# Fetching edge lists a slot earlier, releasing slots exactly, and adding three bf16 parts in PSUM, in a graph attention kernel on one core

## The reference

```python
def _gat_layer(x, W, al, ar, b, src, dst, apply_act):
    h = (x @ W).reshape(N_NODES, HEADS, HEAD_DIM)
    el = einsum('nhd,hd->nh', h, al); er = einsum('nhd,hd->nh', h, ar)
    e = leaky_relu(el[src] + er[dst], 0.2)
    ex = exp(e - segment_max(e, dst)[dst])
    a = ex / segment_sum(ex, dst)[dst]
    out = segment_sum(h[src] * a[:, :, None], dst) + b
    return leaky_relu(out, 0.01) if apply_act else out
```

## Time and profile before

| what | value |
|---|---|
| median of 3 runs | 9250.0 us (9241.39 to 9254.71) |
| the profiled execution | 9270.94 us, span of its instructions 9269.2 us |
| PE busy, PEld, DVE, ACT, POOL | 65%, 50%, 51%, 18%, 49% |
| mean granted clock of TensorE | 0.80 |
| pairs of layer 0, 1, 2 | us 182 to 2930, 2955 to 5645, 5673 to 9210 |
| L358 gathers | x4716, 4542.2 us busy on POOL |
| L1285 aggregation | x10560 matmuls, 3761.3 us on PE |
| L992 msg, L1000 sel, L979 sum of parts | 1658.2, 906.2, 466.5 us on DVE, x1320 each |

### The profile page before, as it was taken

The page is one execution under the profiler, slowest core; times in us unless marked ns, Lnnn a source line. Parts: engine busy times, 40 slices in busy tenths (PEclk is TensorE's granted clock), DMA queues, the critical chain, the costliest instruction groups (busy, mean ns, idle before and its releaser), DMA issues.

```text
span 9269.2 us, 139557 instructions
## 1 busy us (share of the span) xinstructions
PE 6004.1 (65%) x27934; PEld 4636.2 (50%) x27935; DVE 4741.8 (51%) x10724; ACT 1700.8 (18%) x4763; POOL 4543.3 (49%) x4723
## 2 busy tenths in 40 slices
PE   4555555555665555555565665566777778888888
PEld 2334434444444344444444453345556666767777
DVE  5445555555555445555555564454544444444444
ACT  2000000000110000000000000012333444445454
POOL 1655555555554665555555554555444433333332
PEclk8677778778787677777777776678888999999999
DMA  5444444434443444444443444443333322222221
GB/s 177 114 111 111 111 108 113 106 103 104 108 107 95 116 111 113 109 108 111 107 111 99 104 108 95 110 110 93 90 87 79 80 74 72 69 68 66 64 61 43
DMA packets 638573, 909.79 MB, mean 98 GB/s; under 512 B 271425, under 2 KB 484554, under 8 KB 638410
## 3 DMA queue, kind: packets, MB, share of 16 engines
q0 software_dynamic: 226368, 676.39, 28.6%
q1 hardware_dynamic: 369546, 192.99, 8.8%
q10 hardware_dynamic: 42624, 40.02, 1.3%
HBM read 868.05 MB, written 40.87 MB: 98 GB/s over the span
## 4 chain that ended last, share of the span: by engine, by line
issue 21%; PE 20%; DMA 13%; SPq 12%; DVE 10%; DVEq 10%; another core or an unknown queue 9%; ACT 3%; ACTq 2%; POOL 1%; POOLq 0%
DMA dstb<-dst_d 13%; PE bank L1285 10%; SPq L332 5%; PE bank L1211 5%; PE bank L1222 3%; DVEq L241 3%; DVE msg L992 2%; SPq L334 2%; DVEq L980 2%; DVE sel L1000 2%; DVE selT L968 1%; SPq L326 1%; SPq L340 1%; ACT region L444 1%
## 5 line engine op out<-in xcount | busy, mean ns | idle before, releaser
L358 POOL DMA_INDIRECT gat<-table,meta x4716 | 4542.2, 963 | 4636.2 <-SPq L340 3066.4
L1285 PE MATMUL bank<-msg,sel 128*128 x10560 | 3761.3, 515 | 2365.0 <-DVE sel L1000 1708.3
L1285 PEld LDWEIGHTS bank<-msg,sel 128*128 128x128 f32 x10560 | 2522.7, 251 | 3020.6 <-issue 2516.7
L992 DVE SCALAR_TENSOR_TENSOR msg<-bank,gat 128x1056 f32 x1320 | 1658.2, 1256 | 856.7 <-ACT bank L487 636.9
L1000 DVE TENSOR_TENSOR sel<-iota_t,meta 128x512 f32<-128x512 f32 x1320 | 906.2, 686 | 775.2 <-remote 459.4
L487 ACT ACTIVATE bank<-lg 128x32 f32<-128x32 f32 x1320 | 261.3, 198 | 5476.9 <-DVE lg L986 3750.5
L979 DVE TENSOR_REDUCE lg<-bank 128x64 f32<-128x192 f32 x1320 | 466.5, 353 | 849.6 <-remote 607.7
L1257 PEld LDWEIGHTS bank<-uvb,selT 128*128 128x128 bf16 x5292 | 329.7, 106 | 1121.0 <-issue 563.3
L1257 PE MATMUL bank<-uvb,selT 128*128 (+1 forms) x5292 | 390.4, 195 | 748.2 <-DVE selT L968 490.0
L984 DVE TENSOR_TENSOR lg<-gat,lg 128x64 f32<-128x64 f32 x1320 | 299.3, 227 | 967.4 <-issue 520.6
L1211 PE MATMUL bank<-xT,w 128*128 128x128 f32 x6272 | 782.6, 279 | 16.1 <-issue 16.0
(11 more groups left out here) (188 smaller groups left out, 2133.1 us busy)
## 6 DMA issues: line engine op xcount, KB each, us to landing
dstb<-dst_d SPq DMA_DIRECT2D x1179, 128.0 KB
gat<-table,meta POOLq DMA_INDIRECT x4716
meta<-in_edges SPq DMA_DIRECT2D x1179, 4.0 KB
table<-hrow ACTq DMA_DIRECT2D x98, 140.0 KB
w<-in_W SPq DMA_DIRECT2D x2, 4096.0 KB
table<-hrow SPq DMA_DIRECT2D x49, 140.0 KB, 1.8
region<-xnT_d ACTq DMA_DIRECT2D x50, 128.0 KB
region<-qT_d ACTq DMA_DIRECT2D x50, 128.0 KB
```

Source lines behind the costliest of these rows:

```text
L358: pool.indirect_dma_start(gat[:, r, c, :], None, table[l], bass.IndirectOffsetOnAxis(meta[:, r, c, 0:1].bitcast(U32), 0)).then_inc(s_done, 16)
L992: dve_v.scalar_tensor_tensor(msg[:, bass.ds(n % 2, 1), :, :].rearrange("p a c (h d) -> p (a c) h d", h=H), ex_p.unsqueeze(3).to_broadcast( ...
L1285: last = pe.matmul(acc[:, 0:MSG], sel[:, c, :], msg[:, bass.ds(m % 2, 1), c, :].rearrange("p a m -> p (a m)"), start=opens and c == 0, sto ...
```

## The change

It has two parts. In the first, the ring of `meta` gets eight buffers (LISTS) where `dstb` and `gat` keep four, and SP's loop body becomes `fetch`: it waits for `selT` of the pair four slots back (which frees `dstb`), issues `dstb` and then `meta`, and only then waits for `sel` of that pair, and for the landings. AHEAD rises from 4 to 6 with the counts that go with it. The first RING slots of each tile from tile 1 on are fetched with the shift of the tile before. GpSimd's loop runs over eight slots a round instead of four, and the count of slots is rounded for that. In the second, in layers 0 and 1, `prepare` issues three matmuls of 16 columns per chunk that accumulate in PSUM, and DVE's L979 and its drain are left out; L984 reads PSUM, and `iota_t` of a tile's first pair is computed after L984. Layer 2 keeps the old form. `small` shrinks from 512 to 256 columns.

```diff
+LISTS = 2 * RING
-        meta = sb("meta", [P, RING, CH, 2], I32)
+        meta = sb("meta", [P, LISTS, CH, 2], I32)
-        AHEAD = RING
+        AHEAD = RING + 2
+        def tile_shift(eng, T):
+            return eng.value_load(ctl[0:1, bass.ds(T, 1), 3:4].rearrange("a b c -> a (b c)"), min_val=0, max_val=TOTAL_MAX)
@@ sync
+                def fetch(g, shift, start, first):
+                    edge = edges_of(g, start, first)
+                    landed = sp.snap(16 * g)
+                    sp.wait_ge(selT_ready[l], g + shift + 1)
+                    sp.sem_inc(slot_taken, 1)
+                    sp.dma_start(dstb[:, bass.ds(g % RING, 1), :]..., dst16_d[bass.ds(edge, SLOT)]...).then_inc(dst_in[l], 16)
+                    sp.dma_start(meta[:, bass.ds(g % LISTS, 1), :, :]..., a["edges"][...]).then_inc(meta_in[l], 16)
+                    rows_left = sp.snap(g + shift + 2)
+                    sp.wait_ge(msg_ready[l], rows_left)
+                    sp.sem_inc(slot_taken, 1)
+                    sp.wait_ge(meta_in[l], landed)
+                    sp.wait_ge(dst_in[l], landed)
+                    sp.sem_inc(meta_ready[l], 1)
+                start, unshared, last, shift, first = tile_loads(sp, 0)
+                with sp.Fori(unshared, last + 1) as g:
+                    fetch(g, shift, start, first)
+                with sp.Fori(1, NT) as T:
                     start, unshared, last, shift, first = tile_loads(sp, T)
-                    with sp.Fori(unshared, last + 1) as g:
-                        sp.wait_ge(msg_ready[l], g + shift)
-                        ... meta, then dstb, then both waits, then meta_ready
+                    shift_before = tile_shift(sp, T - 1)
+                    with sp.Fori(unshared, first + RING) as g:
+                        fetch(g, shift_before, start, first)
+                    with sp.Fori(first + RING, last + 1) as g:
+                        fetch(g, shift, start, first)
@@ gpsimd
-                    for j in range(RING):
-                        before, r = (j + 1) % RING, (j + 2) % RING
-                        pool.wait_ge(meta_ready[l], RING * i + j + 2)
+                    for j in range(LISTS):
+                        m, before, r = (j + 2) % LISTS, (j + 1) % RING, (j + 2) % RING
+                        pool.wait_ge(meta_ready[l], LISTS * i + j + 2)
@@ vector
-                dve.sem_inc(selT_ready[l], AHEAD)
+                dve.sem_inc(selT_ready[l], AHEAD - 1)
                 selectT(1, 0, selT_first[l])
+                dve.drain()
+                dve.sem_inc(selT_ready[l], 1)
                     dve.wait_ge(uv_ready[l], n)
-                    dve_v.tensor_reduce(lg2[:], uv_p[...], AX.X, ALU.add)
-                    dve.drain()
+                    looked_up = uv_p[:, 0:CH * UV].rearrange("p (c w) -> p c w", w=UV)
+                    if l + 1 == LAYERS:
+                        dve_v.tensor_reduce(lg2[:], uv_p[...], AX.X, ALU.add)
+                        dve.drain()
+                        looked_up = lg2[:]
                     dve.wait_ge(gathered[l], g)
-                    dve_v.tensor_tensor(lg2[:], rows_of(g)[:, :, MSG:ROW], lg2[:], ALU.add)
+                    dve_v.tensor_tensor(lg2[:], rows_of(g)[:, :, MSG:ROW], looked_up, ALU.add)
@@ tensor
+                        else:
+                            for k in range(PARTS):
+                                last = pe.matmul(uv_p[:, c * UV:(c + 1) * UV], selT[:, c * P:(c + 1) * P],
+                                                 uvb[:, bass.ds(T, 1), k:k + 1, :]..., start=k == 0, stop=k + 1 == PARTS)
```

More of the change, by code:

```diff
@@ L135, in build @@
         ctl = sb("ctl", [1, NT, CTL], I32)
-        small = sb("small", [P, 512])
+        small = sb("small", [P, 256])
         ismall = sb("ismall", [P, 64], I32)
@@ L322, in _ @@
                                      ).then_inc(seg_meta[l], 16)
-                with sp.Fori(0, NT) as T:
-                    start, unshared, last, shift, first = tile_loads(sp, T)
-                    with sp.Fori(unshared, last + 1) as g:
-                        edge = edges_of(g, start, first)
-                        r = g % RING
-                        sp.wait_ge(msg_ready[l], g + shift)
[L331 to L340, removed]
+                def fetch(g, shift, start, first):
[3 more added lines that the diff above has]
+                    sp.sem_inc(slot_taken, 1)
+                    sp.dma_start(dstb[:, bass.ds(g % RING, 1), :].rearrange("p a e -> p (a e)"),
+                                 dst16_d[bass.ds(edge, SLOT)].rearrange("(a e) -> a e", a=1).to_broadcast([P, SLOT])
+                                 ).then_inc(dst_in[l], 16)
+                    sp.dma_start(meta[:, bass.ds(g % LISTS, 1), :, :].rearrange("p a c w -> p (a c w)"),
+                                 a["edges"][bass.ds(2 * edge, SLOT * 2)].rearrange("(p f) -> p f", p=P)).then_inc(meta_in[l], 16)
+                    rows_left = sp.snap(g + shift + 2)
[4 more added lines that the diff above has]
+                    sp.sem_inc(meta_ready[l], 1)
@@ L355, in _, with gather_row @@
             for l in range(LAYERS):
-                def gather_row(r, c, s_done):
+                def gather_row(m, r, c, s_done):
                     pool.indirect_dma_start(gat[:, r, c, :], None, table[l],
-                                            bass.IndirectOffsetOnAxis(meta[:, r, c, 0:1].bitcast(U32), 0)
+                                            bass.IndirectOffsetOnAxis(meta[:, m, c, 0:1].bitcast(U32), 0)
                                             ).then_inc(s_done, 16)
@@ L700, in _ @@
             dve_v.tensor_tensor(ring, slots_before, share, ALU.subtract)
[L701 to L702 removed]
+            dve_v.tensor_scalar(ismall[0:NT, 4:5], slots_all, -1.0, float(LISTS * TOTAL_MAX + 1), ALU.mult, ALU.add)
+            dve_v.tensor_scalar(ismall[0:NT, 5:6], slots_all, float(LISTS - 2), None, ALU.add)
             dve.drain()
[L704 to L705 removed]
+            dve_v.tensor_scalar(ismall[0:NT, 4:5], ismall[0:NT, 4:5], LISTS - 1, None, ALU.bitwise_and)
+            dve_v.tensor_scalar(out_ctl[:, 9:10], ismall[0:NT, 5:6], LISTS.bit_length() - 1, None, ALU.logical_shift_right)
             dve.drain()
@@ L1000, in select @@
                     dve_v.tensor_tensor(sel[:], iota_t[:].unsqueeze(1).to_broadcast([P, CH, P]),
-                                        meta[:, bass.ds(g % RING, 1), :, 1:2].rearrange("p a c w -> p (a c) w").to_broadcast([P, CH, P]),
+                                        meta[:, bass.ds(g % LISTS, 1), :, 1:2].rearrange("p a c w -> p (a c) w").to_broadcast([P, CH, P]),
                                         ALU.is_equal).then_inc(msg_ready[l], 1)
@@ L1256, in prepare @@
                     for c in range(CH):
-                        last = pe.matmul(uv_p[:, c * PARTS * UV:(c + 1) * PARTS * UV], selT[:, c * P:(c + 1) * P],
-                                         uvb[:, bass.ds(T, 1), :, :].rearrange("p a k w -> p (a k w)"), start=True, stop=True)
+                        if l + 1 == LAYERS:
+                            last = pe.matmul(uv_p[:, c * PARTS * UV:(c + 1) * PARTS * UV], selT[:, c * P:(c + 1) * P],
+                                             uvb[:, bass.ds(T, 1), :, :].rearrange("p a k w -> p (a k w)"), start=True, stop=True)
+                        else:
+                            for k in range(PARTS):
+                                last = pe.matmul(uv_p[:, c * UV:(c + 1) * UV], selT[:, c * P:(c + 1) * P],
+                                                 uvb[:, bass.ds(T, 1), k:k + 1, :].rearrange("p a k w -> p (a k w)"),
+                                                 start=k == 0, stop=k + 1 == PARTS)
                     last.then_inc(uv_ready[l], 1)
```

18 lines of the change are left out of this document (10 added, 8 removed).

## The result

The changed kernel takes 9762.06 us (9750.05 to 9790.68, 4 runs) against 9252.35 us before (4 runs): a ratio of 1.0533, 95% interval 1.05 to 1.0565. It is slower by 5.3%, where 1.4% faster was forecast.

A forecast was written before the change was run, and what follows sets the result against it. SP's loop over lists, engaged 94 and 97% of layers 0 and 1, was taken as the bound. -90 + 170 - 190 + 0 - 15 = -125 us took 9269 to 9144, about 9125 for the runs' median; range 8850 to 9400 us.

The forecast's parts named there:

- What bounds the kernel: Layers 0 and 1: SP's loop over lists is a limit, by turns with DVE and PE; 6.25 us sets the pace.
- caps what any help elsewhere can give: SP, free only 6% and 3% of layers 0 and 1, limits other gains to 242 us unless its loop shortens.
- my three signs of being wrong: DVE's remote waits up over 125 us, SP's fetch over 6.6 us on average, or the `dstb` landing leaving the chain.
- the second rival: List latency as true limit: hidden `dstb` landings give -450 us, 8800 us; much faster, chance 15%.
- The fetch and the header: SP: reordered fetch saves 0.1 us on 876 fetches, -90 us; longer tile header in layers 0 and 1 costs +170 us.
- the waits: SP in layers 0 and 1: earlier lists and exact release remove 80% of 242 us waiting, -190 us (-100 to -242).
- some -25 us: Layer 2: 0.1 us saved on about 90 early fetches, and -15 us from half of DVE's later gather waits.
- The sum on TensorE: Layers 0 and 1: shorter DVE step only brings releases forward, extra matmuls are hidden; 0 us, bounds -100 and +100.
- The uncovered price: PE's extra small matmuls, if not hidden behind `msg` and `sel`: 260 to 700 us over 880 pairs.
- The credit of the same part: DVE loses L979 and the idleness after it: 880 × 0.6 = 530 us of work goes, counted as 0 in time.
- more gathering stalls VectorE: Fewer GpSimd pauses lengthen DVE's remote waits: centre 9365 us (growth by a third), 9485 by half; slower, chance 24%.

The follow-up runs named there:

- e1: The changed kernel with VectorE's sum kept in all layers (lists early and exact release alone): 9300.52 us, ratio 1.0029 to the kernel before.
- c3: Lists early and exact release alone, VectorE's sum kept, run again in a later session: ratio 1.0065 to the kernel before.
- c6: Lists early and exact release alone, VectorE's sum kept, one more repetition: ratio 1.0041 to the kernel before.
- e3: The kernel before plus eight unused 16-column matmuls per pair in layers 0 and 1, VectorE's sum kept: 9575.94 us, ratio 1.0329.
- c7: The kernel before plus two unused 256-column matmuls per pair in layers 0 and 1, in stepping conditions: 9299.76 us, ratio 1.0041.
- e2: The kernel before with only the sum moved to TensorE (twelve accumulating matmuls per pair, layers 0 and 1): 9554.17 us, ratio 1.0307.
- e4: The kernel before plus a drain and eight one-column exps per pair on ScalarE in layers 0 and 1, quick conditions: 7762.9 us, ratio 1.0022.
- e5: The kernel before plus two unused 256-column matmuls per pair in layers 0 and 1, quick conditions: 7685.9 us, ratio 0.9922.
- g1: The kernel before with one gather per slot instead of four, quick conditions: 7620.01 us, ratio 0.9846.
- g2: The kernel before with one gather per slot and eight additional 16-column matmuls per pair in layers 0 and 1, quick conditions: 7534.95 us, ratio 0.9733.

## Why the prediction was wrong

**What bounds the kernel.** SP's loop did bound the first tile and shared the rest. The step from there to a cap on everything else ("caps what any help elsewhere can give") holds for gains alone. I then used it as if it also kept harm away. The agreement that seemed to confirm SP as the pace was none: 6.25 us is a time per fetch, 6.24 us one per pair, and per fetch layer 0 takes 2748 / 393 = 6.99 us. Two of my three signs of being wrong came: the remote waits grew by more than 125 us, and the landing left the chain, though with a loss and not with the second rival's gain.

**The fetch and the header** (-90 + 170) and **the waits** (-190): for the lists alone the sum was -125 us. Measured: +27, +60 and +38 us (e1, c3, c6 by their ratios). Up to the end of layer 1 the direction was right, -48 us in e1 where my terms give about -100. SP's waits for the release fell there from 242.4 us to 148.2 (`sel` 145.4, `selT` 2.8), by 94 and not by 190. In layer 2, where I gave some -25 us, e1 lost 65: DVE's wait for exp (`msg` on ACT) rose from 595.2 to 880.1 us.

```profile
DVE msg L992 <- ACT bank L487: 595.2, 176, 14.0
...
DVE msg L1012 <- ACT bank L503: 880.1, 200, 13.2
```

In the kernel's order ScalarE's exp stands behind the experts' work. Why earlier lists make it later was not tried.

**The sum on TensorE** (0, bounds -100 and +100) is the step that failed. I priced twelve matmuls by their busy time, 0.3 to 0.8 us more per pair, and hid it behind `msg` and `sel`. The busy time is even smaller, 0.51 us for twelve in the timeline above against 0.26 for four, and the cost of this part alone was +3.07% and +3.03%, 280 us, nearly three times the bound. e3 shows where it comes from: the eight additional matmuls bring it with VectorE's sum kept, and DVE's late hand-overs from PE grow by 816 us. The uncovered price that I wrote down, 260 to 700 us, would have held it, but as TensorE's own time in front of the aggregation; c7, with as much of that time in two instructions, cost 33 us, an estimated 183 at most without the help of the clock. What the runs show in its place is a cost that goes mostly with the number of matmuls and arrives as late hand-overs. The credit of the same part failed as well: 530 us less DVE work was worth 22 us, because DVE then waited the longer for PE.

**The rival "more gathering stalls VectorE"** named the right symptom, remote waits at these two lines, and 9365 us, with 9485 for growth by half. They doubled, and the time came out 277 us above even that. Its cause never came about: GpSimd's pauses for SP grew (678.4 and 617.1 to 877.9 and 922.5 us), with lists alone they stayed (1365.5 us in the two layers against 1332.7), and so did the remote waits (565.9 + 530.0 against 1067 us). The waits were in front of me; I asked only what would lengthen gathering, and not how many more hand-overs would be late with more matmuls.

**The 189 us that only both halves cost** can be placed. They are not in DVE's remote waits, which add up: in layers 0 and 1 these grow by 28 us in e1, by 937 in e2 and by 979 in the changed kernel. They are at `msg`, which waits for ScalarE's exp: 88 us before, 123 in e1, 114 in e2 and 336 in the changed kernel, 187 more than the halves together. In layer 1 ScalarE copies a turned tile of the linear attention once per tile (L541, now L557) and only then takes up the next exp. Its waits for PE there, before and changed:

```profile
ACT region L541 <- PE bank L1172: 228.1, 37, 9.6
ACT region L541 <- issue: 82.6, 12, 8.2
...
ACT region L557 <- remote: 501.6, 41, 16.1
```

Before, e1 and e2 wait there 311, 308 and 309 us in all, the changed kernel 553 us, and its two repetitions 582 and 563. One case, PE's transposes, then ScalarE, then DVE:

```profile
4634.95 0.27 PE L1195 MATMUL bank<-kc,region 128*128 128x128 f32 x1
...
4644.24 0.38 ACT L557 ACTIVATE region<-bank 128x256 f32<-128x256 f32 x1 [15.33 <-remote]
4644.52 0.20 ACT L503 ACTIVATE bank<-lg 128x32 f32<-128x32 f32 x1
4644.93 1.26 DVE L1015 SCALAR_TENSOR_TENSOR msg<-bank,gat 128x1056 f32 x1 [10.20 <-issue]
```

PE was done at 4635.22, ScalarE went on 9.0 us later, 1.4 us after the last of an unbroken run of gathers, and DVE stood 10.20 us for it. No run took this wait away, so that it is the 189 us is read from the traces and not tested.

**What stays open**: why this hand-over is late only with both halves, and what makes the steps and the late hand-overs.

Instruction fetch hardly changed: 14 packets on q8 after, 13 before. So the rule of the Trainium skill ("Runtime: NRT & Kernel Launch", Instruction fetch mechanics) that a branch out of the fetched window costs a fetch doesn't explain the loss.

## What to carry to other kernels

Where the waits of an engine are put down to something remote, and plain queue instructions take many times their median, price an instruction by its number as well as by its busy time: here a split of one matmul into three cost more than the vector work that it saved. Before calling added work free, look whether the clock rose and paid for it. A bound on the gain (an engine that is 94 to 97% engaged) is no bound on the loss. Compare a variant only with runs of the same session: the same kernel stood at 9250 and at 7747 us, and two wide matmuls a pair lost 0.4% in one session and won 0.8% in the other.

## What the runs showed of the hardware that I had not expected

The same kernel ran at 9250 and at 7740 us in different sessions, steadily within each. What differs in the traces is the 0.70 us steps (SP's move takes 29 ns in every one of 1179 cases of e4, up to 1.4 us in the changed kernel) and the hand-overs put down to something remote (none in e4 and e5, up to 17.1 us long in the stepping conditions). In three of the long ones that I looked at (17.09, 3.57 and 15.33 us) the waiting engine went on 1.4 to 2.1 us after the last of an unbroken run of gathers; such runs are there in the quick conditions too, without the waits, so the gathers alone don't make them.

In the quick conditions additional TensorE work won time, and the granted clock rose with it: 0.881 in g1, 0.899 in g2 with eight small matmuls more per pair.

```profile
core 0: 7618.4 us, clock 0.881
...
core 0: 7563.1 us, clock 0.899
```
